# A two-layer image kernel: softmax weights divided in TensorE while they are turned, and a last stage with four buffers and whole rows

## The reference

```python
# layer 0, per image: 49 windows of 8x8 pixels, 4 heads of 32 channels, 4 chosen windows of 49
x   = x + dwconv3x3(x)
qkv = layernorm(x) @ qkv_w + qkv_b
k_sel, v_sel = the 4 windows with the largest q_win . k_win      # 256 pixels per window
att = softmax(einsum('bpqhd,bpkhd->bphqk', q * SCALE, k_sel))    # 64 x 256 per window and head
o   = einsum('bphqk,bpkhd->bpqhd', att, v_sel)
x   = x + (o + dwconv5x5(v)) @ wo_w + wo_b
x   = x + gelu(layernorm(x) @ w1 + b1) @ w2 + b2
# layer 1
y   = conv3x3(x); xr = mamba(y as sequences of 8 tokens of 16)
out = x + silu(groupnorm(xr, 4 groups) * gn_w + gn_b)
```

## Time and profile before

| what | value |
|---|---|
| median of 3 runs | 10985.12 us (10958.4 to 10985.89) |
| the profiled execution | 10976.78 us |
| its span, first to last instruction | 10974.7 us |
| mean granted TensorE clock | 0.897 |
| image stage | about 0 to 4470 us |
| second stage | about 4470 to 10637 us |
| last stage | 10637 to 10974.7 us |

### The profile page before, as it was taken

One profiled execution on the slowest core, in us unless ns is written; L12 is line 12 of the kernel. 1 busy time (PEld: TensorE's weight loads), 2 busy tenths in 40 slices (PEclk: granted clock), 3 DMA queues, 4 the chain that ended last, 5 costly groups with the idle time before them and its releaser, 6 DMA issues. The chain is left out here.

```text
span 10974.7 us, 195169 instructions
## 1 busy us (share of the span) xinstructions
PE 8590.6 (78%) x61658; PEld 3670.2 (33%) x61658; DVE 9186.9 (84%) x11368; ACT 5945.0 (54%) x10997; POOL 6007.1 (55%) x3646
## 2 busy tenths in 40 slices
PE   5888888888888888778777777788777777787850
PEld 3554544544444445222222222222222222222210
DVE  7777777777777777699999999999999999999974
ACT  4555555555555555555555555555555555555533
POOL 2222222222222222487788788887887877878750
PEclk9999999999999999888889898888898888889875
DMA  2222222222222222111111111111111111111139
GB/s 65 66 66 66 66 66 66 66 66 66 66 66 66 66 66 69 43 37 34 36 36 37 35 36 35 37 35 36 36 38 34 38 34 36 36 36 36 35 69 233
DMA packets 865726, 590.60 MB, mean 54 GB/s; under 512 B 622704, under 2 KB 725104, under 8 KB 860496
## 3 DMA queue, kind: packets, MB, share of 16 engines
q1 hardware_dynamic: 761424, 423.61, 17.0%
q0 software_dynamic: 49152, 100.76, 2.5%
q10 hardware_dynamic: 54016, 51.91, 1.6%
HBM read 109.27 MB, written 103.81 MB: 19 GB/s over the span
## 5 line engine op out<-in xcount | busy, mean ns | idle before, releaser
L1136 POOL TENSOR_TENSOR b_hh<-b_hh,b_cn 128x1024 f32<-128x1024 f32 x1600 | 3832.5, 2412 | 1034.3 <-DVE b_hh L1391 1033.4
L1391 DVE TENSOR_TENSOR_SCAN b_hh<-b_dA,b_ub 128x512 f32<-128x512 f32 x3200 | 3864.8, 1208 | 0.0
L1260 ACT ACTIVATE b_dA<-b_db,b_negA 128x448 f32<-128x448 f32 x3200 | 1976.6, 633 | 1736.0 <-PE b_db L1485 1717.8
L267 POOL DMA_DIRECT2D kvsel<-kv x1536 | 1103.0, 721 | 3188.5 <-issue 2408.6
L1383 DVE TENSOR_TENSOR b_ub<-b_ub,b_bn 128x512 f32<-128x512 f32 x3200 | 2173.0, 679 | 360.8 <-PE b_ub L1485 343.8
L1485 PE MATMUL b_ub<-b_rows,b_pick 96*64 96x512 bf16 x6400 | 1401.6, 439 | 988.1 <-DVE b_hh L1391 947.2
L1485 PE MATMUL b_db<-b_rows,b_pick 96*64 96x512 bf16 x6400 | 1266.0, 419 | 218.9 <-ACT b_dA L1260 215.5
L1485 PEld LDWEIGHTS b_ub<-b_rows,b_pick 96*64 96x64 bf16 x6400 | 358.4, 110 | 3172.6 <-DVE b_hh L1391 2523.7
L522 DVE SCALAR_TENSOR_TENSOR oacc<-vpad,vec,oacc 128x1064 f32<-128x1064 f32 (+1 forms) x934 | 1197.9, 1299 | 11.4
L383 ACT ACTIVATE prob<-score,nmax 128x256 f32<-128x256 f32 (+1 forms) x1600 | 735.5, 471 | 818.1 <-DVE nmax L493 726.9
L1521 PE MATMUL b_acc<-b_hh,b_gather 64*32 64x512 f32 x12800 | 1046.1, 716 | 2.8 <-POOL b_hh L1136 2.8
(11 more groups left out here) (179 smaller groups left out, 12057.2 us busy)
## 6 DMA issues: line engine op xcount, KB each, us to landing
b_rows<-b_term SPq DMA_DIRECT2D x2400, 64.0 KB, 2.0
kvsel<-kv SPq DMA_DIRECT2D x1600, 64.0 KB, 2.0
kvsel<-kv POOLq DMA_DIRECT2D x1536, 64.0 KB, 2.0
xpad<-in_x SPq DMA_DIRECT2D x18, 1568.0 KB, 10.6
ys<-ysb ACTq DMA_DIRECT2D x16, 1600.0 KB, 8.6
b_yc<-ys SPq DMA_DIRECT2D x100, 256.0 KB, 2.7
xr<-b_xo SPq DMA_DIRECT2D x100, 256.0 KB, 2.1
x<-x3pad SPq DMA_DIRECT2D x16, 1568.0 KB, 18.1
```

The lines of the kernel that those rows point to most:

```text
L267: eng.dma_start(kvsel[:, slot, j, :, WPIX * t:WPIX * (t + 1)].unsqueeze(1), kv[:, bass.ds(at[t], 1), :, :]).then_inc((s_kv, s_kg)[j][slot] ...
L1136: nc.gpsimd.tensor_tensor(out=now, in0=now, in1=cn[:, par, :].unsqueeze(1).broadcast_to([C, 2, HT]), op=ALU.mult).then_inc(s_pm, 1)
L1260: nc.scalar.activation(later(dA[:, k % DEEP, :]), later(db[k % 2][:, :]), ACT.Exp, scale=negA[:, 8 * q + e:8 * q + e + 1]).then_inc(s_a, 1)
L1391: nc.vector.tensor_tensor_scan(hh[:, k // 2 % PDEEP, HT * (k % 2):HT * (k % 2 + 1)], dA[:, k % DEEP, :], ub[(UNITS * par + k) % 3][:, :], ...
```

## The change

In the image stage VectorE no longer multiplies `prob` by the reciprocals. It writes four diagonal matrices `scaled` (one per head: the identity times the reciprocal of each row), in one instruction. TensorE then multiplies `prob` by `scaled` where it multiplied by the identity, in a plain matmul instead of a transpose. `scaled` has two buffers, and a new wait holds its writing until the turn of two pairs before has ended.

In the last stage there are four buffers, and the DRAM tensor `xr` is laid out by channel, so that an image's row is contiguous; three loads take the place of four. The store of the second stage writes into that layout. VectorE's order in the last stage is changed: `scales(b)`, then `moments(b + 1)`, then `total(b)`.

```diff
+        scaled = sb("scaled", [C, 2, HEADS, C])
...
                 dve.wait_ge(s_ri, ONE + n + 1)
-                for h in range(HEADS):
-                    now = prob[rows(p), u, h]
-                    m = nc.vector.tensor_scalar(out=now, in0=now, scalar1=rinv[rows(p), u, h:h + 1], scalar2=None,
-                                                op0=ALU.mult)
-                m.then_inc(s_nm, 1)
+                if p >= 2:
+                    dve.wait_ge(s_pt, ONE + n - 1)
+                k = WPIX * wins(p)
+                nc.vector.tensor_tensor(out=scaled[rows(p), u, :, 0:k],
+                                        in0=ident[rows(p), 0:k].unsqueeze(1).broadcast_to([k, HEADS, k]),
+                                        in1=rinv[rows(p), u].unsqueeze(2).broadcast_to([k, HEADS, k]),
+                                        op=ALU.mult).then_inc(s_nm, 1)
...
-                                m = nc.tensor.transpose(turn[:, 2 * h + c, rows(p)], prob[rows(p), u, h, C * c:C * (c + 1)],
-                                                        ident[rows(p), rows(p)])
+                                m = nc.tensor.matmul(turn[:, 2 * h + c, rows(p)], prob[rows(p), u, h, C * c:C * (c + 1)],
+                                                     scaled[rows(p), u, h, rows(p)], start=True, stop=True)
...
-                sp.dma_start(xr_dram[bass.ds(n, 1)].rearrange("a c g p -> c (a g) p"), xo[:, :, :]).then_inc(s_os, 16)
+                sp.dma_start(xr_dram[:, :, bass.ds(n * CPX, CPX)], xo[:, :, :]).then_inc(s_os, 16)
...
-        S = 2
+        S = 4
...
             def body(b, q, g, u):
-                sp.wait_ge(s_res, ONE + FREE + b - 1)
-                chunk = xr_dram[bass.ds(q * CHUNKS, CHUNKS), :, g, :].rearrange("j c p -> c j p")
...
+                sp.wait_ge(s_res, ONE + FREE + b - (S - 1))
+                seq = xr_dram[:, g, bass.ds(q * SPX, SPX)]
+                sp.dma_start(xr[0:64, u, 0:PIX - WPIX], seq[0:64, 0:PIX - WPIX]).then_inc(s_x[u], 16)
+                sp.dma_start(xr[0:64, u, PIX - WPIX:PIX], seq[64:128, 0:WPIX]).then_inc(s_x[u], 16)
+                sp.dma_start(xr[64:128, u, :], seq[64:128, WPIX:SPX]).then_inc(s_x[u], 16)
...
+            moments(0, 0, 0)
+            with dve.Fori(0, NB - 1) as q:
+                for g in range(G):
+                    b = q * G + g
+                    scales(b, g)
+                    moments(b + 1, q + (g + 1) // G, (g + 1) % G)
+                    total(b, g)
+            for g in range(G):
+                b = IMGS - G + g
+                scales(b, g)
+                if g + 1 < G:
+                    moments(b + 1, NB - 1, g + 1)
+                total(b, g)
...
-    xr_dram = nc.dram_tensor("xr", (NB * CHUNKS, C, G, CPX), FP32).ap()
+    xr_dram = nc.dram_tensor("xr", (C, G, NB * SPX), FP32).ap()
```

More of the change, by code:

```diff
@@ L1622, in sem @@
             return sems[-1]
-        red = [ctx.enter_context(nc.psum_tensor(f"c_red{i}", [C, 2], FP32)) for i in range(2)]
-        S = 2
+        red = [ctx.enter_context(nc.psum_tensor(f"c_red{i}", [C, 2], FP32)) for i in range(4)]
+        S = 4
         vec = sb("vec", [C, NV])
@@ L1641, in normalise @@
         s_w = sem("w")
-        s_x = [sem("x0"), sem("x1")]
+        s_x = [sem(f"x{i}") for i in range(S)]
         s_st = sem("st")
@@ L1649, in normalise @@
         s_res = sem("res")
-        s_out = [sem("out0"), sem("out1")]
+        s_out = [sem(f"out{i}") for i in range(S)]
         def v(name):
             return vec[:, _V[name][0]:_V[name][0] + 1]
-        N_W, LOADS, STATS = 2, 6, 9
+        N_W, LOADS, STATS = 2, 5, 9
         FREE = S
@@ L1661, in images @@
                 for g in range(G):
-                    body(q * G + g, q, g, g % 2)
+                    body(q * G + g, q, g, g)
         @block.sync
@@ L1720, in body @@
                 act.wait_ge(s_sc, ONE + 3 * b + 3)
-                act.wait_ge(s_out[u], ONE + 32 * (2 * q + g // 2 + 1))
+                act.wait_ge(s_out[u], ONE + 32 * (q + 1))
                 nc.scalar.activation(res[:, u, :], xr[:, u, :], ACT.Silu, bias=shift[:, u], scale=sc[:, u]
@@ L1727, in _ @@
             for x in s_out:
-                act.wait_ge(x, ONE + 32 + 32 * IMGS // 2)
+                act.wait_ge(x, ONE + 32 + 32 * NB)
         @block.vector
@@ L1733, in _, with moments @@
             nc.vector.memset(eps[:, :], EPS_GN)
-            def body(b, q, g, u):
-                dve.wait_ge(s_x[u], ONE + 16 * LOADS * (2 * q + g // 2 + 1))
+            def moments(b, q, u):
+                dve.wait_ge(s_x[u], ONE + 16 * LOADS * (q + 1))
                 for j in range(7):
@@ L1746, in body, with scales @@
                                                in1=mv[:, u, 1:2], op0=ALU.mult, op1=ALU.add).then_inc(s_st, 1)
+            def scales(b, u):
                 dve.wait_ge(s_red, ONE + b + 1)
@@ L1761, in body, with total @@
                                         ).then_inc(s_sc, 1)
+            def total(b, u):
                 dve.wait_ge(s_act, ONE + b + 1)
@@ L1764, in body @@
                                         ).then_inc(s_res, 1)
-            images(dve, body)
+            moments(0, 0, 0)
[11 more added lines that the diff above has]
+                total(b, g)
 TAP_PAIRS = ((0, 1), (2, 3), (None, 0), (1, 2), (3, None))
```

## The result

The median went from 10985.12 us (10955.19 to 10996.05, five runs) to 10912.14 us (10904.59 to 10918.66, five runs): a ratio of 0.9941, interval 0.9923 to 0.9959. The profiled execution took 10918.66 us around a span of 10916.9, which is 58 us less than before.

What follows compares the result with a forecast made beforehand. The image stage was taken as bound by a ring of TensorE, VectorE and ScalarE, the last stage by DMA. Savings of 46 us and 18 us sum to 64, giving a median of about 10921 us, range 10840 to 10995.

Steps and rivals of the forecast that it cites:

- Turning, TensorE: Image stage: eight transposes become 16 product instructions at 0.108 us, 1.74 us a turn, 0.87 more.
- rival A: Image stage: TensorE's products cost more, no gain above 0.122 us each; 11135 or 11465 us; chance 0.10.
- The ring after: Image stage, engines waiting on each other: four rounds 20.04 instead of 20.92 us, 0.22 a round, 4.4 an image.
- rival C: Image stage gains 0 because handovers eat the saving, last stage -18; 10967 us; chance 0.18.
- Start of each attention: Image stage, first pairs at half clock: the turn costs 1.75 us more, the share 0.7 less; 1.5 lost in all.
- Rival B: Image stage: fewer waits keep the clock up, start costs nothing, 0.3 us a round gained; 10871 us; chance 0.20.
- The last rounds: Image stage, end of each attention: rounds taking 4.48 us now come out at 4.47.
- Loads of the last stage: Last stage: loads go from 180 to 213 GB/s, 8.9 to 7.5 us an image, saving 22 us.
- rival D: Last stage: whole rows of xr are read no faster than 180 GB/s; 10943 us; chance 0.10.
- Four buffers: Last stage: buffers would fill DMA gaps, but there is none before 10955 us, so nothing gained.
- The end: Last stage: new order adds 6 us from last landing to end, less 2: +4; 29 us from landing to end.
- Store of the second stage: Second stage: 2 KB rows become four of 512 bytes; cost nothing, or 100 us if the cover went.

Runs made afterwards that it cites:

- run 4: Four buffers and VectorE's new order in the last stage, old layout with 512-byte pieces, against the kernel before: 10985.24 us, ratio 0.9989.
- run 3: New layout of xr with whole rows and one load fewer, two buffers and old order, against the kernel before: 10975.96 us, ratio 0.9985.
- run 5: Whole rows and four buffers in the last stage, VectorE's old order kept, against the kernel before: 10920.76 us, ratio 0.9933.
- run 2: The second stage's store and whole last-stage edit alone (whole rows, four buffers, new order), against the kernel before: 10955.89 us, ratio 0.9964.

## Why the prediction was right, and where it was not

The verdict and the total were right, with the image stage forecast 20 us too good and the last stage 20 us too bad. That the total came within 9 us is luck, and neither stage gained by the path that was forecast alone: the image stage gained by the clock, and half of the last stage's gain is from buffers priced at nothing. By its own steps:

- *Division, VectorE.* Right: 681 ns against 679, and the maximum starts 0.61 us after the share (forecast 0.63).
- *Turning, TensorE.* Mechanism right, size off: "on 128 columns 0.108". It measured 0.118. A possible reason is that a weight load (196 ns here) hides behind 448 columns but not wholly behind 128; no run isolated it. The turn is 1.89 us, 0.15 over the forecast. The price stays just under the 0.122 at which rival A began. The factor of 4 that the Trainium skill, "TensorE: Matmul & The Clock Gate", section Terms, gives the transpose mode for float32 is not seen: 0.90 us became 1.89, a factor of 2.1.
- *The ring after.* The kinds of rounds came near: the merge round 5.78 (forecast 5.72), plain rounds 4.54 and 4.56 (4.47), the two-tap round 5.60 (5.38), TensorE's wait under 200 us. The term did not: "0.22 us a round, some 20 rounds an image: 4.4 us" is nothing at the same clock, 102.3 us for twenty rounds before and 102.5 after. The longer products took 0.15 us a round of it, and the period that was walked was not typical: it took 20.92 us where the mean of before at full clock is 20.5. At an equal clock the ring closed at no gain, which is rival C.
- *Start of each attention.* Wrong: the 1.5 us was not lost. The first four rounds took 22.8 us before and 21.5 after, 1.3 less, at a mean clock of 0.76 and 0.80. The last twenty took 103.7 and 102.5, 1.2 less, because the clock stayed up. Rival B had this mechanism (a start that costs nothing, no falls in the middle), not its size: 2.5 us an image where it counted 6.
- *The last rounds.* "4.48 now, come out at 4.47" left out the turns behind the last maximum, which nothing hides: from the last maximum to the start of the last product of `attend` it was 9.6 us in every image and is 10.9. The whole rest of an image grew by 1.0 us in the mean. Together: 2.5 less in attention, 1.0 more behind it, 1.6 an image or 25 us.
- *Loads of the last stage.* Right: 27 us alone against 22, the 180 GB/s is gone; rival D fell. So did C's last stage of -18.
- *Four buffers.* The step that failed. "They would fill DMA gaps, but there is none" took a busy share of 1.08 for a full DMA. The engines were busy with packets that a mix would have moved faster: 220 GB/s for loads alone, 384 for a store beside loads. Buffers with the new order brought 22 us before their cost at the end (run 4); with whole rows and the old order they brought 31 (270.1 us in run 3, 238.9 in run 5).
- *The end.* Right: 28.4 us against 29 forecast, 4.9 more than before. But the new order also costs on the way, 13 us between the profiles of runs 2 and 5, which the prediction had not priced: "that starves nobody" was true and beside the point.
- *Store of the second stage.* No cost seen in before and after: the 3200 multiplications of its line 1383 (1386 in after) run for 6092.3 and 6092.2 us from first to last. Over all profiles they take 6078 to 6114 us with the old layout and 6091 to 6113 with the new, so a cost of a few us would not show.

## What to carry to other kernels

When work moves from one engine of a ring to another, price both halves on their own: here minus 12 and plus 11 us an image left 1.6, and that came with the clock. Compare rounds at the same granted clock before calling them shorter. A DMA share of 1 says that packets are in flight, not that the bytes could not move faster: compare the GB/s of stretches with different mixes, and keep enough buffers that loads are queued whenever a store goes out. After a change that loads one engine, look for work that the relieved one can take back; one tap moved to VectorE and the plain order in the last stage together gave another 0.4 to 0.6% here (10866.72 against 10912.14 us, 0.9881 against 0.9941, on two chips).

## What the runs showed of the hardware

- Loads alone move 213 to 221 GB/s on this core with 12.5 KB rows, and 180 with 512-byte pieces in the mix; a store beside them brings the sum to 382 and 384 in the two windows, up to 436 in single microseconds. Loads from two queues do not add: 247 GB/s.
- At full clock one instruction of a float32 product of 128 columns with new stationary data costs 0.118 us, and a product is two of them; a transpose costs 0.113 us (eight in 0.90 us) and is one.
- In the last twenty rounds of an attention the granted clock was 0.967 before and 1.000 after (means of 16 attentions), and at 1.00 in both the rounds took the same time, 102.3 and 102.5 us.
- A multiply of 128x512 whose two operands are both read with zero steps costs 681 ns, the same as one on plain data (679).
